# Shift rows moved from SyncE's to ScalarE's DMA queue, denominators gathered a step later, reciprocals double-buffered

## What is computed

```python
K = heads(x @ Wk + bk)            # 16 heads of 16
V = heads(x @ Wv + bv)            # 16 heads of 64
scores = einsum('bhqd,bhkd->bhqk', heads(x), K) + causal_mask
o = einsum('bhqk,bhkd->bhqd', softmax(scores), V)
y = layernorm(x + (x + gelu(o) @ Wf + bf))
h = silu(y @ wg) * (y @ wu)       # 768 wide, integer weights / 127
out = layernorm(y + h @ wd)
```

## Time and profile before

| | us |
|---|---|
| three runs | 2195.44, 2197.97, 2216.67 |
| median | 2197.97 |
| the profiled execution's own time | 2213.07 |
| its span | 2211.1 |
| mean granted TensorE clock in it | 0.928 of full |
| busy, share of the span: PE, DVE, POOL, ACT | 88%, 68%, 51%, 47% |
| bytes moved | 303 MB, all on SP's queue but 0.9 MB |

### The profile page before, as it was taken

The page is one execution under the profiler, slowest core; times in us unless marked ns, Lnnn a source line. Parts: engine busy times, 40 slices in busy tenths (PEclk is TensorE's granted clock), DMA queues, the critical chain, the costliest instruction groups (busy, mean ns, idle before and its releaser), DMA issues. The chain is left out here.

```text
span 2211.1 us, 38994 instructions
## 1 busy us (share of the span) xinstructions
PE 1935.3 (88%) x10304; PEld 999.6 (45%) x10304; DVE 1496.8 (68%) x3598; ACT 1044.7 (47%) x1523; POOL 1128.5 (51%) x1192
## 2 busy tenths in 40 slices
PE   5799988988997898999888999977879889999996
PEld 4344434444443343444333344322336667666664
DVE  3786767767685776767676767765736767767764
ACT  1155444544554454454445545533544545545543
POOL 0186666666676666665666676664751212212212
PEclk9699999999999999999999999887989999999998
DMA  8434334343433434343343434362126465575530
GB/s 285 152 129 153 135 128 163 111 146 128 154 132 122 163 115 149 120 161 134 121 158 120 150 120 156 111 193 98 66 59 152 136 179 130 155 179 133 163 105 20
DMA packets 257657, 303.12 MB, mean 137 GB/s; under 512 B 24736, under 2 KB 174368, under 8 KB 257584
## 3 DMA queue, kind: packets, MB, share of 16 engines
q1 hardware_dynamic: 257584, 302.24, 43.0%
HBM read 174.20 MB, written 127.93 MB: 137 GB/s over the span
## 5 line engine op out<-in xcount | busy, mean ns | idle before, releaser
L930 ACT ACTIVATE weights<-ring 128x1024 f32<-128x1024 f32 (+3 forms) x768 | 601.4, 809 | 498.9 <-PE ring L677 488.8
L647 POOL TENSOR_TENSOR weight_sum<-weight_sum,weights 128x512 f32<-128x512 f32 (+3 forms) x448 | 681.9, 1522 | 9.6
L677 PE MATMUL o_acc<-weights,v_pair 128*64 128x512 f32 (+3 forms) x3072 | 647.6, 531 | 12.5 <-POOL weights L625 9.7
L677 PE MATMUL ring<-q_stack,k_stack 50*128 50x512 f32 (+3 forms) x1536 | 322.6, 425 | 163.1 <-DMA q_stack<-shifts 117.9
L625 POOL TENSOR_SCALAR_AFFINE_SELECT weights<-weights 128x256 f32<-128x256 f32 x512 | 219.2, 431 | 417.6 <-ACT weights L930 414.7
L1080 DVE TENSOR_REDUCE part_max<-ring 128x2 f32<-128x1024 f32 x256 | 303.6, 1207 | 137.7 <-PE ring L677 137.5
L1088 DVE CUSTOM_DVE_ANT_0 scrap<-ring,causal 128x128 bf16<-128x128 f32 (+3 forms) x512 | 230.6, 488 | 232.8 <-PE ring L677 231.2
L668 POOL TENSOR_TENSOR h_lo<-hidden,h_hi 128x512 f16<-128x512 f32 x96 | 114.5, 1194 | 446.1 <-ACT h_hi L898 446.1
L677 PE MATMUL ring<-k_stack,q_stack 48*128 48x512 f32 (+3 forms) x1536 | 317.1, 416 | 25.8 <-DMA k_stack<-k_rows 16.7
L677 PEld LDWEIGHTS ring<-q_stack,k_stack 50*128 50x128 f32 x1536 | 153.8, 197 | 380.5 <-issue 128.9
L677 PEld LDWEIGHTS o_acc<-weights,v_pair 128*64 128x64 f32 x3072 | 180.7, 143 | 252.6 <-issue 222.2
(11 more groups left out here) (105 smaller groups left out, 2199.7 us busy)
## 6 DMA issues: line engine op xcount, KB each, us to landing
v_pairs<-v_unit SPq DMA_DIRECT2D x64, 512.0 KB, 4.9
v_pair<-v_pairs SPq DMA_DIRECT2D x64, 512.0 KB, 4.4
o_heads<-o_pair SPq DMA_DIRECT2D x64, 512.0 KB, 5.4
g<-o_heads SPq DMA_DIRECT2D x16, 2048.0 KB, 19.3
den_wide<-reciprocals SPq DMA_DIRECT2D x32, 1024.0 KB, 13.0
q_stack<-q_rows SPq DMA_DIRECT2D x128, 192.0 KB
k_stack<-k_rows SPq DMA_DIRECT2D x128, 192.0 KB
q_rows<-x_hi SPq DMA_DIRECT2D x32, 512.0 KB, 5.5
```

What stands on the lines that cost most here:

```text
L647: pool.tensor_tensor(dst, other, W[t][:, :, :], ALU.add).then_inc(s_add, 1)
L677: return nc.tensor.matmul(o, l, r, start=start, stop=stop)
L930: nc.scalar.activation(W[t][:, :, :], bank_of("t", t)[:, :, 0:width_of(t)], ACT.Exp).then_inc(s_w, 1)
```

## The change

Four edits, which come together:

1. `move_shifts` and `load_shifts` go from SP's list to ACT's: the same six DMAs, issued by ACT after the exponents of burst 1 and of burst 3. On DVE `shift_turn` moves from behind the second score tile to behind the first.
2. The denominators are gathered (`load_den`) one step later, ahead of that step's own stores; the reciprocals move from burst 2 of that step to burst 5 of the step after it, and are stored another step later (the last ones behind the loop). The loop gets one more step.
3. A second buffer for the widened reciprocals, `dn[1]`, on the memory of the Q stacks, so that its first load waits until all `scoreT` are done. In `finish` the order is now `load_g`, then `load_dn`, and `load_dn(r+2)` waits only for `norm(r)`.
4. `norm(0)` is spread over steps 60 to 63, two slices at burst 6 of each, in place of eight slices in step 65.

```diff
-        dn = sb("den_wide", [P, HC, U], F32)
+        dn0 = sb("den_wide0", [P, HC, U], F32)
...
+        qctx = ExitStack()
+        Q = [sb(f"q_stack{i}", [HSTEP + SROWS + SHROWS, S], F32R, qctx) for i in range(RING)]
+        qctx.close()
+        dn = [dn0, sb("den_wide1", [P, HC, U], F32)]
...
-        STEPS_B = PAIRS + 4
-        LOOP_B = (STEPS_B, 8, 4, UNITS - ALONE - 3)
+        STEPS_B = PAIRS + 5
+        LOOP_B = (STEPS_B, 12, 4, UNITS - ALONE - 4)
...
@@ SP, attend
-                if 1 <= r <= PAIRS:
-                    move_shifts(r - 1, n - 1)
-                if 1 <= r <= PAIRS:
-                    load_shifts(r - 1, n - 1)
...
+                if r % 4 == 3 and 7 <= r < 4 * GROUPS + 7:
+                    load_den((r - 7) // 4 + it)
                 if 3 <= r < PAIRS + 3:
                     store_o(r - 3, n - 3)
                     store_den(r - 3, n - 3)
-                if r % 4 == 2 and 6 <= r < 4 * GROUPS + 6:
-                    load_den((r - 6) // 4 + it)
-                if r % 4 == 3 and 7 <= r < 4 * GROUPS + 7:
-                    store_rec((r - 7) // 4 + it)
+                if r % 4 == 1 and 9 <= r < 4 * GROUPS + 9:
+                    store_rec((r - 9) // 4 + it)
...
-                if r == PAIRS + 1:
+                if r == PAIRS + LEAD:
+
+                    sp.wait_ge(s_st, NS * PAIRS)
                     load_dn(1, 0)
...
@@ SP, load_dn
-                if r >= 1:
-
-                    sp.wait_ge(s_gn, HC * n)
+                if r >= 2:
+
+                    sp.wait_ge(s_gn, HC * (n - 1))
...
@@ SP, finish
                 if r + 2 < UNITS:
+                    load_g(r + 2, it)
+                if r + 2 < UNITS:
                     load_dn(r + 2, it)
-                if r + 2 < UNITS:
-                    load_g(r + 2, it)
...
@@ ACT
+            def move_shifts(n):
+
+                act.wait_ge(s_shs, n + 1)
+                settle(act, s_passed["act"])
+                for i in range(P // SQ):
+                    act.dma_start(sd[...][:, i],
+                                  shiftT[SQ * i:SQ * (i + 1), :].bitcast(F32)).then_inc(s_shd, 16)
+
+            def load_shifts(r, n):
+
+                act.wait_ge(s_shd, 16 * (P // SQ) * (n + 1))
+                settle(act, s_passed["act"])
+                for h in range(2):
+                    row = HSTEP * h + SROWS
+                    act.dma_start(Q[r % RING][row:row + SHROWS, :].bitcast(F32), ...)
...
+                    if 1 <= r <= PAIRS and b == 1:
+                        move_shifts(n - 1)
+                    if 1 <= r <= PAIRS and b == 3:
+                        load_shifts(r - 1, n - 1)
...
@@ DVE, attend
                         if what == "s" and j == 0 and 1 <= r <= PAIRS:
                             shift_lo(r - 1, n - 1)
-                        if what == "s" and j == 1 and 1 <= r <= PAIRS:
                             shift_turn(r - 1, n - 1)
+                    if b == 6 and PAIRS - 4 <= r < PAIRS:
+                        norm(0, 0, range(2 * (r - PAIRS + 4), 2 * (r - PAIRS + 5)))
...
-                    if b == 2 and k == 3 and 7 <= r < 4 * GROUPS + 7:
-                        reciprocals((r - 7) // 4 + it, r == 7)
-                if r == PAIRS + 1:
-                    norm(0, 0, range(HC))
-
+                    if b == 5 and k == 0 and 8 <= r < 4 * GROUPS + 8:
+                        reciprocals((r - 8) // 4 + it, r == 8)
```

More of the change, by code:

```diff
@@ L157, in build @@
         RING = 4
-        Q = [sb(f"q_stack{i}", [HSTEP + SROWS + SHROWS, S], F32R) for i in range(RING)]
+        qctx = ExitStack()
+        Q = [sb(f"q_stack{i}", [HSTEP + SROWS + SHROWS, S], F32R, qctx) for i in range(RING)]
+        qctx.close()
+        dn = [dn0, sb("den_wide1", [P, HC, U], F32)]
         K = [sb(f"k_stack{i}", [HSTEP + SROWS + SHROWS, S], F32R) for i in range(RING)]
@@ L224, in build @@
         s_wrest = sem("ffn_weights_ready")
-        s_passed = {e: sem(f"passed_{e}") for e in ("sp", "pool", "pe", "dve")}
+        s_passed = {e: sem(f"passed_{e}") for e in ("sp", "act", "pool", "dve")}
         s_xt = sem("xt_loaded")
@@ L262, in build @@
         s_xn = [sem(f"xn_loaded{i}") for i in range(2)]
-        s_dn = sem("den_wide_loaded")
+        s_dn = [sem(f"den_wide_loaded{i}") for i in range(2)]
         s_gn = sem("g_normalised")
@@ L432, in store_o @@
                              osb[r % 2][:]).then_inc(s_ost[r % 2], 16)
[L434 to L449, removed]
             def store_den(r, n):
@@ L539, in load_dn @@
                 n = r + 2 * it
-                if r >= 1:
-                    sp.wait_ge(s_gn, HC * n)
+                if r >= 2:
+                    sp.wait_ge(s_gn, HC * (n - 1))
                     settle(sp, s_passed["sp"])
                 for h in range(2):
-                    sp.dma_start(dn[DV * h:DV * (h + 1)], rd[bass.ds(b, 1), h:H:2, t0:t0 + U].rearrange(
-                        "o c t -> (o c) t").partition_broadcast(DV)).then_inc(s_dn, 16)
+                    sp.dma_start(dn[r % 2][DV * h:DV * (h + 1)], rd[bass.ds(b, 1), h:H:2, t0:t0 + U].rearrange(
+                        "o c t -> (o c) t").partition_broadcast(DV)).then_inc(s_dn[r % 2], 16)
             load_x(0, True)
@@ L575, in _ @@
             walk(sp, *LOOP_B, attend)
+            store_rec(GROUPS - 1)
             for i in range(2):
@@ L952, in gelus @@
                                          bias=bv_sb[:, c:c + 1]).then_inc(s_gelu, 1)
+            def move_shifts(n):
+                act.wait_ge(s_shs, n + 1)
+                settle(act, s_passed["act"])
+                for i in range(P // SQ):
+                    act.dma_start(sd[bass.ds(n, 1)].rearrange("o h m (u s q) -> (o h m u) s q", s=P // SQ, q=SQ)[:, i],
+                                  shiftT[SQ * i:SQ * (i + 1), :].bitcast(F32)).then_inc(s_shd, 16)
[4 more added lines that the diff above has]
+                    row = HSTEP * h + SROWS
+                    act.dma_start(Q[r % RING][row:row + SHROWS, :].bitcast(F32),
+                                  sd[bass.ds(n, 1), h].rearrange("o m t -> (o m) t")).then_inc(s_shl[r % RING], 16)
             def attend(r, it):
@@ L1140, in norm @@
                     if c == 0:
-                        dve.wait_ge(s_dn, 32 * (n + 1))
+                        dve.wait_ge(s_dn[r % 2], 32 * (r // 2 + it + 1))
                         dve.wait_ge(s_g[r % 2], 16 * (r // 2 + it + 1))
-                    v.tensor_tensor(g[r % 2][:, c], g[r % 2][:, c], dn[:, c], ALU.mult).then_inc(s_gn, 1)
+                    v.tensor_tensor(g[r % 2][:, c], g[r % 2][:, c], dn[r % 2][:, c], ALU.mult).then_inc(s_gn, 1)
             def attend(r, it):
```

## The result

| | before | after | forecast |
|---|---|---|---|
| median, us | 2198.51 (2195.44 to 2216.67) | 2102.36 (2090.24 to 2108.82) | 2095, range 2040 to 2180 |
| ratio | | 0.955, 95% interval 0.9515 to 0.9585 | 0.953 |
| profiled execution / span | 2213.07 / 2211.1 | 2108.82 / 2107.1 | 2109 |

What follows compares the result with a forecast made beforehand. The prediction took PE's waits for late shift rows, held up in SP's queue, as the bound (stage C bound elsewhere). Terms -139 - 12 + 5 + 42 = -104 us gave 2109 us profiled, 2095 by the median's scale, range 2060 to 2150, 8 in 10 within 2040 to 2180.

Steps and rivals of the forecast that it cites:

- What bounds the kernel: Stage B: PE loses 117.9 us waiting for shift rows, late because SP's stores land behind its own three-engine stack loads.
- Part 1, the step: Pairs 4 to 56: moving shift DMAs to ACT shortens each of 52 steps from 24.17 to 21.5 us, gaining 139 us.
- ACT's delay: Stage B steps: issuing the shift DMAs on ACT adds 0.4 us a step, bounds 0 and 2.6.
- The term of 21.1 for a step without waits: Stage B: mean of four full-clock steps, two counted whole and two by PE's busy time only, 21.1 us a step.
- Part 1, the landing: Stage B: shift store lands about 1.1 us after its last issue, within ACT's 4.0 us of room, so no wait.
- the third rival: Stage B: store still lands behind stack loads, over 4.0 us after ACT's last issue; +127 us, 2324 us, chance 0.08.
- Step 58: Shifts pass stage C's loads, but the stack comes some 6 us late; 12 us gained, bounds 0 and 21.
- Part 2: Stage B: gathering denominators a step later costs and brings nothing once the shifts are on ACT's queue.
- Part 4 and the tail: End of stage B: half of norm(0)'s slices on the path, 3 us off for a faster end; +5 us, bounds -5 and +15.
- Part 3: Stage C: norm starts 2.0 us later in each of 14 cycles, with more half clock; +42 us, bounds 0 and 60.
- The 14 us for the half clock: Stage C: longer PE idling makes norm 1.5 us slower in some 9 cycles, 14 us within the +42.
- The first rival: Stage C loses nothing because its loads end as early as before; 2053 us by the median's scale, chance 0.15.

Runs made afterwards that it cites:

- Experiment 6: Kernel before with every 48-row stack load cut into three of 16 rows, shifts staying on SP; 2035.2 us, ratio 0.9245.
- experiment 1: Kernel before with only the six shift DMAs of a step moved to ACT and DVE's transpose behind the first score tile; 2074.5 us, ratio 0.9442.
- experiment 3: Changed kernel with norm(0) in one piece in step 65 again; 2091.05 us, ratio 0.9507 to the kernel before.
- experiment 2: Kernel before with only the second buffer of widened reciprocals and load_g ahead of load_dn in finish; 2210.2 us, ratio 1.0044.
- experiment 8: Kernel before with den_wide loaded from 64 distinct rows of o_heads, same bytes, output not the reference's; 2158.1 us, ratio 0.9789.
- experiment 11: Kernel before with stack loads cut into 16-row DMAs and the shift DMAs moved to ACT, DVE's transpose earlier; 2122.3 us, ratio 0.9641.

## Why the prediction was right, and where it was not

**What bounds the kernel**: right. The rows were late because SP stood behind its own stack loads on three engines. Experiment 6 spreads these loads, and the waits go with it (117.9 to 6.4 us). The text had the cause in hand (3/16 = 0.19) and priced only the change's way around it.

**Part 1, the step**: right in kind, 27 us too much. Of the 0.52 us by which the step of 22.02 is above 21.5, part 2 has 0.18 by the changed kernel and experiment 1. ACT's delay was put at 0.4 and measured 0.35 without part 2 and 0.52 with it. The term of 21.1 for a step without waits leaned on taking all idle time of two of four rows as wait; experiment 6, where PE waits neither for shifts nor for ACT, has 21.21, so this is 0.1 us of the miss. Beyond ACT's 0.35 us, a step of experiment 1 is another 0.28 longer than one of experiment 6: PE is busy 0.17 us more (1093.4 against 1084.5 us in the 52 steps) and waits 0.07 more for DVE. Why PE is busy longer is open.

**Part 1, the landing**: "a few such rows cost well under 1 us" was wrong, and so was "the wait is 0". The store lands 4.6 us after the last issue ends (5.0 after it starts), not 1.1 with a little on top; the bound of 4.0 us for a loss was passed. ACT's list stands at the load until the landing in 51 of 52 steps, which is near to the sign given for the third rival. It cost little, because the next work of ACT waits for PE's product anyway; the landing ended ACT's wait last in only four steps (7.5 us). The third rival's condition was met by 0.6 us and its price was not, since its price hung on 14 us. On the page "DMA: Bandwidth & Descriptors" of the Trainium skill, both sections weighed hold something. By "Queues, rings and completion order" the store passes the stack loads, and it does: by the medians of the traces it lands 1.7 us ahead of their last packet, where before it landed 1.4 us behind it. By "Issuing engines are not separate DMA queues" it shares the engines with them, and is still slowed (5.0 us against 1.3 in experiment 6); but more than issue time is saved. Not all of the step from 9.95 to 5.0 us is passing: the store is also issued later behind the first stack load, 7.8 us in place of 5.4.

**Step 58**: as written, the shifts pass and the stack comes late, by 7.9 us where 6 were forecast. The stretch gives 7.5 us and not 12 mostly because the first two `norm` slices of part 4 lie in it: without them, in experiment 3, it gives 10.5.

**Part 2**: "it costs and brings nothing" holds to some 6 us, and only as worded, once part 1 is in. Alone it brings 54 us, the same SP time gained another way. Parts of one change that relieve one queue must not be priced each alone.

**Part 4 and the tail**: +12.7 in place of +5, within the bounds. PE waits for nearly all of the slices, not half: 2.9 us in each of four steps, and experiment 3 gives 11.3 us. The 3 us taken off for a faster end of stage B were not there. The +3.5 us of the last row belong to part 3, as experiment 2 has them too.

**Part 3**: this step failed. +42 was forecast; the two profiled executions differ by +0.5, and experiment 2 gives some 10 us, which the lengths of stage C in the other experiments bear out. The order in SP's list and the later start were read rightly, and so was the wait's new name. Wrong was "the engines are full, so the sum of the transfers is unchanged". Full engines move 153 GB/s or 378, by what they carry, and a load of one row 64 times costs less behind `g` than ahead of it (204 against 153 GB/s). So the next `norm` starts on average 0.2 us later behind the end of the one before it (21.2 against 21.0 us), not 2.0. The row of 245 GB/s at a share of 0.99 was a mean over both and hid it; cut in two windows it would have shown. That `den_wide` is slower at the head of the burst from the reciprocals than from distinct rows is shown (experiment 8); why the order matters, and why it stays at half the rate of `g`, is not. The 14 us for the half clock stood on the same step and came to some 5: the 14 norms together take 182.5 to 185.9 us in the three kernels with the new order, 176.5 to 181.1 in the five with the old order that experiment 2 names.

The first rival ("stage C loses nothing", 2053) was thus nearer on its stage, 10 us off where the forecast is 32 off, and would have been wrong on the total by 49 us: the steps of stage B and the tail took back what it spared. The near hit of the total is luck: by the profiled executions the errors, 27 + 5 + 8 + 2 (the start) against 42, cancel in the sum. The medians say the same: part 1 brought 124 us and not 151, parts 2 and 4 cost some 6 and 11 and not 0 and 5, part 3 10 and not 42, together -97 for the forecast -104.

## What to carry to other kernels

When a small transfer is late behind a large one, look first at how many DMA engines the large one uses (a share of 0.19 is three): here cutting it into loads of 16 rows took off 7.6%, moving the small one to another engine's queue 5.6%, and both together only 3.6%. Before a stretch of one profiled execution is compared with another's, look whether each lies near its median. A second buffer pays when its load stands ahead of the wait that it was to escape in the list of its queue; here two exchanged lines were worth 51 us. A DMA issued by an engine on the critical path takes some 0.45 us of that engine each, and its gaps take only so many.

## What was not expected of the hardware

- The shift store takes 5.0 us to land on a queue of its own beside 4 KB rows on three engines, 9.95 behind them on the same queue, and 1.3 with the engines free (experiment 6).
- At a DMA share near 1, 2 MB of `den_wide` (each row 64 times, 64 partitions to a DMA) move at 153 GB/s ahead of `g` and 204 behind it, and at 201 from distinct rows (experiment 8); `g` (128 partitions to a DMA) at 373 to 384.
- Four DMA issues on ACT took 1.8 us (median) while the stack loads held three engines, and 2.7 us once these were cut (experiment 11).
- 1.8 us more of issuing on ACT made the step 3.2 us longer and brought the mean clock to 0.936.
